# Where ScalarE's gate, silu and softplus bursts stand in a selective-scan kernel, and three products and two sums given to other engines

## The reference, cut to what matters

```python
x = einsum('bld,ed->bel', ctx, in_proj_w)
x = silu(conv(x, 4 taps, per channel) + conv_b)          # u
dt_low, B, C = split(einsum('bdl,ed->bel', x, x_proj_w))
dt = softplus(dt_low @ dt_proj_w + b)
state = state * exp(dt * A) + (dt * u) * B                # over 512 positions, 16 states
y = sum over states of (state * C) + D * u
y = y * silu(layernorm(x_in))
x1 = x_in + y.T
out = x1 + layernorm(x1) @ sum(factors) / sqrt(8) + bias
```

## Time and profile before

| | us |
|---|---|
| median of 3 runs | 483.63 (482.84 to 483.75) |
| the profiled execution, its own time | 482.48 |
| its span, first to last instruction | 480.7 |

### The profile page before, as it was taken

The page is one execution under the profiler, slowest core; times in us unless marked ns, Lnnn a source line. Parts: engine busy times, 40 slices in busy tenths (PEclk is TensorE's granted clock), DMA queues, the critical chain, the costliest instruction groups (busy, mean ns, idle before and its releaser), DMA issues.

```text
span 480.7 us, 4118 instructions
## 1 busy us (share of the span) xinstructions
PE 432.1 (90%) x1119; PEld 185.3 (39%) x1119; DVE 453.5 (94%) x327; ACT 344.7 (72%) x578; POOL 420.6 (88%) x223
## 2 busy tenths in 40 slices
PE   8799797999979868898989789899979999989996
PEld 5134343434434233333434244343434343344432
DVE  5797999989999999989999999999999899999996
ACT  4669574977659788796869977697879876654422
POOL 4369999998979899997999979797998958999972
PEclk9989999999999989999999999999999999999999
DMA  5799746438982000100694000000396000000002
GB/s 193 267 355 350 200 80 138 83 55 217 292 337 88 1 0 0 42 25 1 191 412 168 0 22 1 0 24 0 132 381 237 1 22 23 22 22 22 0 1 88
DMA packets 16847, 53.96 MB, mean 112 GB/s; under 512 B 1828, under 2 KB 2084, under 8 KB 15800
## 3 DMA queue, kind: packets, MB, share of 16 engines
q1 hardware_dynamic: 15384, 45.14, 25.9%
q0 software_dynamic: 1152, 8.39, 8.8%
q10 hardware_dynamic: 288, 0.18, 0.1%
HBM read 49.24 MB, written 4.46 MB: 112 GB/s over the span
## 4 chain that ended last, share of the span: by engine, by line
POOL 53%; issue 20%; DVE 11%; ACT 6%; PE 4%; DMA 4%; SPq 1%; POOLq 0%; DVEq 0%; ACTq 0%
POOL h L1093 40%; POOL h L1086 9%; DVE dA L946 7%; POOL dtu L1079 3%; DMA c_rep<-bc_scratch 2%; PE y L519 2%; DVE acc L920 2%; ACT dA L776 1%; DMA chan<-channel 1%; DVE h L952 1%; PE work L415 1%; POOL fsum L1123 1%; DVE h L946 1%; ACT gate L690 0%; SPq L331 0%
## 5 line engine op out<-in xcount | busy, mean ns | idle before, releaser
L1093 POOL TENSOR_TENSOR h<-b_rep,dtu 128x1024 f32<-128x1024 f32 x127 | 302.3, 2446 | 12.3 <-DMA b_rep<-bc_scratch 11.3
L519 PE MATMUL y<-h,ident 128*128 128x512 f32 x508 | 236.5, 602 | 34.9 <-DVE h L952 33.0
L946 DVE TENSOR_TENSOR_SCAN dA<-dA,h 128x1024 f32<-128x1024 f32 x97 | 221.8, 2287 | 11.6 <-ACT dA L776 11.1
L776 ACT ACTIVATE dA<-dt,a_neg 128x512 f32<-128x512 f32 x256 | 166.0, 681 | 92.9 <-DVE h L952 76.2
L519 PEld LDWEIGHTS y<-h,ident 128*128 128x128 f32 x508 | 92.8, 190 | 166.2 <-issue 103.7
L952 DVE TENSOR_TENSOR h<-dA,c_rep 128x1024 f32<-128x1024 f32 x96 | 117.1, 1220 | 2.4 <-DMA c_rep<-bc_scratch 0.3
L1086 POOL TENSOR_TENSOR h<-h,c_rep 128x1024 f32<-128x1024 f32 x31 | 74.5, 2403 | 22.3 <-DVE h L946 22.3
L946 DVE TENSOR_TENSOR_SCAN h<-dA,h 128x1024 f32<-128x1024 f32 x31 | 70.6, 2279 | 0.1
L403 PE MATMUL work<-ctx_sb,w_in 128*128 128x512 f32 x60 | 30.6, 644 | 0.3 <-DMA w_in<-w_inT 0.2
L507 PE MATMUL work<-fsum,xnT 128*128 128x512 f32 x64 | 28.8, 592 | 0.0
L920 DVE SCALAR_TENSOR_TENSOR acc<-work,chan,acc 128x511 f32<-128x511 f32 (+2 forms) x30 | 21.6, 731 | 1.3 <-ACT acc L655 1.2
(11 more groups left out here) (128 smaller groups left out, 375.3 us busy)
## 6 DMA issues: line engine op xcount, KB each, us to landing
b_rep<-bc_scratch SPq DMA_DIRECT2D x32, 512.0 KB, 9.7
c_rep<-bc_scratch SPq DMA_DIRECT2D x32, 512.0 KB, 9.3
fsum<-factors POOLq DMA_DIRECT2D x8, 1024.0 KB, 8.3
x<-x SPq DMA_DIRECT2D x4, 1024.0 KB, 7.7
out<-x SPq DMA_DIRECT2D x16, 256.0 KB, 2.0
ctx_sb<-ctxT SPq DMA_DIRECT2D x3, 512.0 KB, 5.7
ctx_sb<-ctxT SPq DMA_DIRECT2D x2, 256.0 KB, 4.4
w_in<-w_inT SPq DMA_DIRECT2D x1, 384.0 KB, 5.2
```

The lines of the kernel that those rows point to most:

```text
L519: mm = pe.matmul(y[:], ident[:], h[:, (s * PAIRS + j) % H_RING, i, :], start=False, stop=(j == sum_order(s)[-1] and i == 1))
L776: act.activation(dA[:, j % 2, i, :], dt[:, k % 2, :], ACT.Exp, scale=a_neg[:, k, 2 * j + i:2 * j + i + 1]).then_inc(exp_done, 1)
L946: dve.tensor_tensor_scan(pair if on_pool(s * PAIRS + j) else decay, decay, pair, 0.0, ALU.mult, ALU.add).then_inc(scanned, 1)
L1093: pool.tensor_tensor(h[:, (s * PAIRS + j) % H_RING], b_rep[:, j], dtu[:, k % 2, :].unsqueeze(1).to_broadcast([P, 2, L]), ALU.mult).then_in ...
```

## The change: what it does

- POOL_C: steps 3, 9 and 11 give one more c product to GpSimd (pair 2; 4; 4); steps 4, 8 and 12 give it pair 4 instead of pair 2. SUM_ORDERS then gives these steps the order that fits.
- Softplus stands in slot 0 in steps 4, 6, 8, 10 and 12 (slot 2 elsewhere).
- silu_batch stands in slot 2 in steps 6 and 10 (still slot 4 in step 2).
- The gate stands in slot 2 in steps 4, 8 and 12. In step 0 it is cut in two bursts of two blocks, in slots 4 and 6, each with its own two table loads. The wait for the buffer is put before blocks 0 and 3 only.
- The statistics of step 2 go from slot 3 to slot 5.
- TENSOR_RESIDUAL takes in steps 4 and 10.
- FIRST_FILL: 6, 0, 2, 2 products with zeros before the four parts of the first projection, and 3 behind it, into a PSUM buffer that isn't in use.

```diff
-POOL_C = ((0, 4), (0,), (0, 2), (0,), (0, 2), (0, 2), (0, 2), (0, 2, 4), (0, 2), (0, 2), (0, 2), (0, 2), (0, 2), (0, 2),
-          (0, 2), (0, 2))
-SOFTPLUS_SLOT = 2
+POOL_C = ((0, 4), (0,), (0, 2), (0, 2), (0, 4), (0, 2), (0, 2), (0, 2, 4), (0, 4), (0, 2, 4), (0, 2), (0, 2, 4), (0, 4),
+          (0, 2), (0, 2), (0, 2))
+SOFTPLUS_SLOTS = (2, 2, 2, 2, 0, 2, 0, 2, 0, 2, 0, 2, 0, 2, 2, 2)
+SILU_SLOTS = {2: 4, 6: 2, 10: 2}
+GATE_BLOCKS = ({4: (0, 1), 6: (2, 3)}, {2: (0, 1, 2, 3)}, {2: (0, 1, 2, 3)}, {2: (0, 1, 2, 3)})
 C_LAG = 3
-TENSOR_RESIDUAL = (0, 1, 2, 6, 8)
+STATS_SLOTS = (5, 3, 5, 3, 5, 3, 3, 3, 5, 3, 3, 3, 5, 3, 3, 3)
+TENSOR_RESIDUAL = (0, 1, 2, 4, 6, 8, 10)
+FIRST_FILL = (6, 0, 2, 2, 3)
...
+            def fill_first(i):
+
+                for _ in range(FIRST_FILL[i]):
+                    pe.matmul(dA[:, 1, 1, :], still[:], ones[:], start=True, stop=True)
+
             def x_proj(b):
                 for k in range(KB):
                     if b == 0:
+                        fill_first(k)
                         pe.wait_ge(u_done, k + 1)
...
             x_proj(0)
+            fill_first(KB)
             pe.wait_ge(w_dt_landed, 16)
...
-            def gate_batch(b):
+            def gate_blocks(b, ks):
 
                 act.wait_ge(g_nb, (b + 1) * KB)
-                if b > 0:
-                    act.wait_ge(gated, b * KB)
-                for k in range(KB):
+                for k in ks:
+                    if b > 0 and k in (0, KB - 1):
+                        act.wait_ge(gated, b * KB - (1 if k == 0 else 0))
                     act.activation(gate[:, k, :], x1_block(b, k), ACT.Silu, bias=g_r[:, 2, k:k + 1],
                                    scale=g_r[:, 1, k:k + 1]).then_inc(g_done, 1)
...
-                    if j == SOFTPLUS_SLOT and is_d:
+                    if j == SOFTPLUS_SLOTS[s] and is_d:
...
-                    if j == (5 if k == 0 else 3) and is_g:
+                    if j == STATS_SLOTS[s] and is_g:
...
-                    if j == 4 and k == 0:
+                    if k == 0 and j in GATE_BLOCKS[b]:
                         act.preload_act_table_set("silu_and_others")
-                        gate_batch(b)
+                        gate_blocks(b, GATE_BLOCKS[b][j])
                         act.preload_act_table_set("natural_log_exp_and_others")
-                    if j == 4 and k == KB - 2 and b + 1 < BATCH:
+                    if k == KB - 2 and b + 1 < BATCH and j == SILU_SLOTS[s]:
                         act.preload_act_table_set("silu_and_others")
                         silu_batch(b + 1)
```

## The result

| us | before | after |
|---|---|---|
| median of 6 runs each | 483.43 (482.84 to 484.42) | 488.69 (485.94 to 489.53) |
| the profiled execution | 482.48 | 489.53 |
| its span | 480.7 | 487.4 |

The ratio of the runs is 1.0096, 95% interval 1.0078 to 1.0113 (the two medians alone give 1.011). The forecast of 474.6 was wrong in sign and the range 471.8 to 479.5 missed it.

What follows compares the result with a forecast made beforehand. VectorE was taken as the bound up to scan (13,0), then an unchanged chain. Gains 3.2 + 0.9 + 4.3 (moved bursts) + 1.4 - 0.8 = 9.0 us gave span 471.7 and median 474.6; range 471.8 to 479.5.

Steps and rivals of the forecast that it cites:

- Three more products on GpSimd: Steps 3, 9, 11: c products leave VectorE, 3.8 us gained less 0.6 for late evacuations, so 3.2.
- residual sums: Steps 4 and 10: two additions of 0.45 us leave VectorE for TensorE, 0.9 gained.
- The rival that GpSimd becomes the bound: GpSimd's leads run out in steps 5 and 12, returning 3.2 us plus 0.6 at (5,6): 478.4 us, chance 0.13.
- Bursts of steps 4 and 8: Moved softplus and gate bursts remove ScalarE stalls: 0.45 us gained in step 4, 1.4 in step 8.
- The rule by which they were placed: A pair's decays may start when the product or GpSimd pair's scan two pairs back is done, and take 1.30 us.
- Bursts of steps 6 and 10: Silu burst of 4.5 us behind pair 2 stalls 0.4 where slot 4 cost 1.12; 0.8 us gained each.
- Step 12: Softplus in slot 0 and gate in slot 2 remove the 1.34 us stall at (12,5): 0.85 gained.
- the rival with the other sign: ScalarE reaches slot 0 of the five burst steps without its lead: slower than before, 485.8 us, chance 0.05.
- VectorE waits for TensorE anywhere: Named sign that the forecast is wrong; no such wait stood between first and last step before, TensorE priced at 0.
- Step 2: Statistics moved from slot 3 to 5 cut the stall at (2,5) from 2.28 us to 0.9: 1.4 gained.
- Step 0's split: Gate in two bursts adds two table loads, 2.6 us, so scan (0,7) starts later: 0.8 lost.
- Fills: First projection: scan (0,0) 0.74 us earlier, lost again at c_rep; 0, bounds 0.7 gained and 0.5 lost.

Runs made afterwards that it cites:

- v_six: Changed kernel, step 12 as before, one gate burst in step 0, t_final in slot 3 in steps 6 and 10, context load ahead of the store: 473.91 us.
- a_silu4: Changed kernel with softplus of steps 6 and 10 back in slot 2 and their silu burst back in slot 4: 479.77 us, ratio 0.9911.
- v_ten: s_both with step 10's softplus in slot 0, silu in slot 2 and block 4's output in slot 3: 476.11 us, ratio 0.9837.
- s_order12: a_silu4 with only step 12's products on GpSimd back to pairs 0 and 2: 479.5 us, ratio 0.9918.
- a_nofill: Changed kernel without the fills of the first projection: 486.99 us, ratio 1.0058 (one run of 1977.83 left out of the ratio).
- v_ten_nofill: v_ten without the fills: 476.57 us, ratio 0.9844.
- b_fill: Kernel before with only the fills of the change added: 483.12 us, ratio 0.9982.
- a_final3: Changed kernel with ScalarE's evacuation of finished rows in steps 6 and 10 moved from slot 2 to slot 3, behind the silu burst: 481.04 us, ratio 0.9936.
- s_gate1: a_silu4 with step 0's gate in one burst in slot 4 again: 477.01 us, ratio 0.9868.
- s_both: Changed kernel with steps 6, 10 and 12 in the order of before and one gate burst in step 0: 476.9 us, ratio 0.9864.

## Why the prediction was wrong, step by step

- **Three more products on GpSimd, 3.2; residual sums, 0.9: right.** Steps 3, 5 and 9 are 1.25, 0.45 and 0.82 shorter. GpSimd's waits for scans fell from 22.3 to 13.8 in the kernel after (which had idle time to give) and to 6.3 in v_six, inside the 6 to 10 named. Its busy time rose by 8.6. The rival that GpSimd becomes the bound is out: the waits of the kernel after name one scan that waits for a b product, for 0.2 us in step 0 (35.94), those of v_six one, for 0.5 us in step 13 (392.57). Its wait in step 13 did not shrink to near 3: it was 5.2 in the kernel after and 4.6 in v_six. The 0.6 that this rival puts at (5,6) did not arise. In step 11 only 1.0 of the forecast 1.5 came in the kernels without the late burst: (11,4) takes 2.89 where I had 2.4.
- **Bursts of steps 4 and 8, 0.45 and 1.4: right**, 0.53 and 1.43. The rule by which they were placed holds, and step 8's walk was exact.
- **Bursts of steps 6 and 10, 0.8 each: wrong, the failing step.** It let the silu burst begin as soon as decays (s,2) end, with t_final at its own 0.6 us at most. The timeline of before shows t_final without idle time ahead of it (200.91), and I read that as no wait. It was a wait covered by what stood in front, the softplus burst that this very change takes away. Its length could have been read there: TensorE's last layer ended at about 200.7, decays (6,2) at 197.7. The sum says 0.8 + 0.8 gained; it was 2.4 + 2.4 lost, and 1.4 more in step 11. These 6.2 us are what a_silu4 gets back by the place of the bursts; the 2.1 of steps 7 and 13 that it gets back too go with half-clock stretches, not with the late bursts from run to run. With t_final behind the burst and the load ahead of the store the same moves earn 1.2 each (v_ten, v_six), more than I gave them.
- **Step 12, 0.85: wrong.** The lead at slot 0 was taken as at step 8. It is 0.76, not about 2, since the step before it got shorter for VectorE and not for the evacuations that wait for TensorE. That is the mechanism of the rival with the other sign, "without its lead", at one of five places and at 1.6 us instead of 2.4 (its own working gives 2.4 less the lead of 0.76, which is 1.6); at the others the lead held, and it isn't what turned the sign.
- **"VectorE waits for TensorE anywhere" was named as what would prove the forecast wrong**, and it did, at (13,1): 2.1 us of step 13, in the stretch behind (13,0) that I had called untouched (95.0 in all, where I had 92.6). POOL_C changes SUM_ORDERS, and I priced the order at nothing. It costs 1.0 at (13,1) (s_order12 against a_silu4), of which 0.6 come back at (13,3), and 1.7 more where a half clock falls on it. Steps 4 and 8 have the same order and no such wait: steps 5 and 9 came out at their forecast.
- **Step 2, 1.4: right**, 1.31. **Step 0's split, 0.8 lost: right**, 0.85. In the kernel after, a load at 51.15 lasts 1.28 and the gate starts at 52.44, 0.01 behind it. The rule of the Trainium skill (ScalarE: Activation LUTs, "What ACT_TABLE_LOAD costs") that puts a switch at about 2.66 us would have made the loss 2.8 higher. The trace doesn't agree with it here: it shows no drain.
- **Fills, 0: right**, within what a measurement tells. The 0.74 that I had named as lost at c_rep is not to be seen: the first scan starts at 24.66 before, 24.98 after and 24.92 in v_ten, with fills, and at 23.97 in a_nofill and 24.18 in v_ten_nofill, without. Only b_fill has it, at 23.93, and one profile of each doesn't part the fills from the spread of the first transfers. Nor do the fills always hold the clock: with them it is at half from 23.0 in v_six.
- **Step 0 ahead of (0,4): 3.3 us in this one profile, open.** In the profiles of a_final3, a_silu4, s_gate1 and s_both, with the same code up to there, (0,4) starts between 41.3 and 42.1, in v_ten at 43.3; before at 41.13, in b_fill at 40.4. So the greater part of the 3.3 us belongs to that execution's transfers; how much of the rest is the change's was not separated. I had not given this any width in the range.

The range was too narrow for one reason above all: each covered wait that a moved burst could bare was priced at zero with no end on the costly side. A bound of "3 us, what TensorE is behind, at each place" was to be read from the rows.

## What to carry to other kernels

An instruction with no idle time ahead of it may still be waiting: before a burst is moved, look for each instruction that stood behind it at when its input was ready, not only at when it started, since the burst may have been its cover. Order in a slot matters more than the slot: what waits for another engine belongs behind the long work that depends on nothing, and whatever a queue issues behind the moved instruction (here SP's next load behind its store) moves with it. A change of which engine makes a product changed here the order in which TensorE sums them, and that order can have a price of its own: 1.0 us at one wait behind step 12, nothing behind steps 4 and 8.

## What the runs showed of the hardware

- A pause of TensorE can be paid more than once, though not each time. In the kernel after, the granted clock is half (1.2 of 2.4 GHz), from step 5 to step 15, in 3.4 us stretches that begin at 191.4, 211.9, 324.5 and 385.9. Each begins 0.3 to 0.6 us after the end of an idle time, of 1.95, 3.06, 3.65 and 2.24 us, and the four products after the last one took 3.45 instead of 1.98. The same idle time drew a half clock in a_final3 too (2.24 us, from 377.2), and none in a_silu4 (2.24) and a_nofill (2.23). What else decides it isn't settled by these runs.
- A 128x4 tensor_scalar on VectorE that takes 0.17 us took up to 1.85 beside a 128x1024 product of GpSimd and ended 0.02 to 0.03 us after it, in after, a_final3, a_silu4, a_nofill, b_fill and v_ten alike; the scan and the batch statistics beside GpSimd's products kept their length. The Trainium skill (GPSIMD Engine Reference, "Specifications") says that GpSimd shares its SBUF interfaces with VectorE and names 2-port modes and two SBUF inputs as the cases that contend; this instruction has one input, and whether it ran in such a mode no run here shows.
